# One piece of the probability split of the last batch on VectorE instead of GpSimd, in a cross-attention kernel

## The reference

```python
q, k, v = heads(layernorm(x) @ w_q), heads(ctx @ w_k), heads(ctx @ w_v)
scores = where(mask, -inf, q @ k.T / 8)
x = x + merge(softmax(scores) @ v) @ w_o
x = x + layernorm(x) @ quantized(kernel) + bias + (layernorm(x) @ a) @ b
```

## Time and profile before

| what | value |
|---|---|
| median of 3 runs | 502.15 us (498.56 to 502.39) |
| span of the profiled execution | 499.3 us |
| busy share of PE, DVE, ACT, POOL | 90%, 81%, 66%, 80% |
| granted TensorE clock, mean | 0.979 of full speed |

### The profile page before, as it was taken

How to read it: one execution, slowest core, us unless ns; L and a number is a source line. 1 busy time by engine, 2 the same in 40 slices (tenths; PEclk the granted TensorE clock), 3 DMA queues, 4 the chain that set the end, 5 groups by cost and what they waited for, 6 DMA issues and landing times.

```text
span 499.3 us, 15466 instructions
## 1 busy us (share of the span) xinstructions
PE 451.8 (90%) x5855; PEld 328.7 (66%) x5855; DVE 406.2 (81%) x1110; ACT 327.6 (66%) x845; POOL 398.7 (80%) x659
## 2 busy tenths in 40 slices
PE   3968989999999999999999999999999999888874
PEld 1434756777766866777766866687667867576662
DVE  4986779987988989788988989898988888778662
ACT  5967566875677766776677766776667666656530
POOL 5687478999788977788788978798797977889931
PEclk9999799999999999999999999999999999899897
DMA  8602685798957996689857985798677877669950
GB/s 284 213 23 43 125 178 113 137 182 169 168 115 144 196 144 118 123 185 161 145 116 141 195 158 119 144 182 160 129 141 128 158 143 142 126 126 177 155 127 27
DMA packets 218817, 71.91 MB, mean 144 GB/s; under 512 B 202785, under 2 KB 216882, under 8 KB 218738
## 3 DMA queue, kind: packets, MB, share of 16 engines
q1 hardware_dynamic: 217680, 69.25, 71.4%
q0 software_dynamic: 480, 1.31, 0.9%
q10 hardware_dynamic: 578, 0.30, 0.2%
HBM read 14.71 MB, written 4.19 MB: 38 GB/s over the span
## 4 chain that ended last, share of the span: by engine, by line
PE 43%; DVE 27%; ACT 16%; POOL 8%; issue 4%; DMA 2%; SPq 0%; DVEq 0%; POOLq 0%; ACTq 0%
PE ps_b L915 32%; ACT arena L673 8%; DVE ps_a L803 7%; PE ps_a L983 6%; DVE arena L796 4%; DVE arena L785 2%; ACT arena L652 2%; DVE arena L871 2%; DMA arena<-in_L_xattn_w_q_dram 2%; POOL arena L580 2%; PE ps_b L1035 2%; POOL arena L584 2%; PE ps_b L1004 2%; ACT arena L664 1%; DVE arena L807 1%
## 5 line engine op out<-in xcount | busy, mean ns | idle before, releaser
L915 PE MATMUL ps_b<-arena 128*128 128x65 f16 (+3 forms) x3348 | 323.6, 249 | 6.1 <-DVE arena L871 3.4
L915 PEld LDWEIGHTS ps_b<-arena 128*128 128x128 f16 x3348 | 224.5, 99 | 81.8 <-issue 6.1
L673 ACT ACTIVATE arena<-ps_a,arena 128x160 f32<-128x160 f32 x512 | 160.0, 396 | 92.6 <-DVE arena L807 84.0
L584 POOL TENSOR_TENSOR arena<-arena 128x512 f16<-128x512 f32 x128 | 148.6, 1161 | 0.0
L580 POOL CAST arena<-arena 128x512 f16<-128x512 f32 x128 | 78.4, 613 | 54.4 <-ACT arena L673 53.1
L803 DVE TENSOR_REDUCE ps_a<-ps_a 128x4 f32<-128x640 f32 x128 | 105.3, 822 | 0.0
L983 PE MATMUL ps_a<-arena 64*128 64x160 f16 x1536 | 76.2, 232 | 13.2 <-ACT arena L673 13.2
L983 PEld LDWEIGHTS ps_a<-arena 64*128 64x128 f16 x1536 | 50.8, 95 | 38.2 <-issue 20.9
L1004 PE MATMUL ps_b<-arena 128*128 128x65 f16 x512 | 72.1, 194 | 0.0
L871 DVE TENSOR_TENSOR arena<-ps_b,arena 128x256 f32<-128x256 f32 x128 | 54.3, 424 | 4.4
L796 DVE TENSOR_TENSOR arena<-ps_b,arena 128x512 f16<-128x512 f32 x60 | 41.1, 686 | 19.1 <-ACT arena L664 17.8
(11 more groups left out here) (139 smaller groups left out, 424.3 us busy)
## 6 DMA issues: line engine op xcount, KB each, us to landing
arena<-in_x_dram SPq DMA_DIRECT2D x8, 512.0 KB, 5.5
mask_u<-in_x_dram SPq DMA_DIRECT2D x32, 128.0 KB, 3.0
out_dram<-mask_u SPq DMA_DIRECT2D x32, 128.0 KB, 2.6
arena<-arena SPq DMA_TRANSPOSE x128, 4.0
arena<-arena SPq DMA_DIRECT2D x24, 65.0 KB, 2.7
arena<-in_L_xattn_w_q_dram SPq DMA_DIRECT2D x1, 1024.0 KB, 8.7
arena<-in_L_xattn_w_k_dram SPq DMA_DIRECT2D x1, 1024.0 KB, 10.7
arena<-in_L_xattn_w_v_dram SPq DMA_DIRECT2D x1, 1024.0 KB, 12.2
```

The source lines that it names most:

```text
L584: nc.gpsimd.tensor_tensor(lo_main, main, hi_main, ALU.subtract)
L673: ins = nc.scalar.activation(probs[k % 2][:, h, :], p_scores[k % 2][:, h % 2, h // 2 * WINDOW:(h // 2 + 1) * WINDOW], ACT.Exp, bias=neg_ma ...
L915: mm = nc.tensor.matmul(dst, a, c, start=(first and at == 0), stop=(last and at == n - 1))
```

## The change

In slots 112 to 127 POOL leaves out the low half of rest. Its split ends with the low half of main, and `p_lo_made` is raised there. DVE makes the low half of rest at the end of its slot k, behind the late items of the slot before. It waits for both high halves of k (`p_hi_made`) and raises a new semaphore, `rest_lo_made`. In these slots SP waits for both semaphores before it turns k, and ACT waits for both of k-2 before it writes `probs`. All other slots are as before.

```diff
+        DVE_RESTS = LAST - NS
             def turn_probs(k):
                 sp.wait_ge(p_lo_made, k + 1)
+                rests_low_by_dve(sp, k)
...
+        def rests_low_by_dve(eng, k):
+            if k >= DVE_RESTS:
+                eng.wait_ge(rest_lo_made, k - DVE_RESTS + 1)
...
                 pool.wait_ge(p_hi_made, 2 * k + 1)
-                nc.gpsimd.tensor_tensor(lo_main, main, hi_main, ALU.subtract)
-                pool.wait_ge(p_hi_made, 2 * k + 2)
-                nc.gpsimd.tensor_tensor(rests[:, :, 2, :], rest, rests[:, :, 0, :], ALU.subtract).then_inc(p_lo_made, 1)
+                ins = nc.gpsimd.tensor_tensor(lo_main, main, hi_main, ALU.subtract)
+                if k < DVE_RESTS:
+                    pool.wait_ge(p_hi_made, 2 * k + 2)
+                    ins = nc.gpsimd.tensor_tensor(rests[:, :, 2, :], rest, rests[:, :, 0, :], ALU.subtract)
+                ins.then_inc(p_lo_made, 1)
...
                     act.wait_ge(p_lo_made, k - 1)
+                    rests_low_by_dve(act, k - 2)
...
+                if DVE_RESTS <= s.k < LAST:
+                    rests = rest_parts(s.k % HALF_BUFS)
+                    dve.wait_ge(p_hi_made, 2 * s.k + 2)
+                    nc.vector.tensor_tensor(rests[:, :, 2, :], probs[s.k % 2][:, :, P:WINDOW], rests[:, :, 0, :],
+                                            ALU.subtract).then_inc(rest_lo_made, 1)
```

More of the change, by code:

```diff
@@ L311, in xattn_ffn @@
         p_lo_made = sem("p_lo_made")
+        rest_lo_made = sem("rest_lo_made")
         turned = [sem(f"turned{i}") for i in range(TURN_BUFS)]
@@ L543, in fast_sp, with rest_parts @@
                 sp.wait_ge(out_stored[i], 16 * (NT // 2 + 1))
+        def rest_parts(i):
+            return p_half[i][:, 2].rearrange("p e (c k) -> p e c k", c=P // REST)
+        def rests_low_by_dve(eng, k):
+            if k >= DVE_RESTS:
+                eng.wait_ge(rest_lo_made, k - DVE_RESTS + 1)
         def gather(b):
@@ L565, in norm @@
                 nc.gpsimd.tensor_tensor(ln_shift, ln_minus, ln_rstd, ALU.mult).then_inc(ln_rstd_made, 1)
-            def rest_parts(i):
-                return p_half[i][:, 2].rearrange("p e (c k) -> p e c k", c=P // REST)
             def split_probs(k):
```

## The result

The changed kernel is slower: 506.77 us in the median of 4 runs (506.41 to 508.34) against 501.79 (498.56 to 502.39), a ratio of 1.0128 with a 95% interval of 1.0089 to 1.0167. I had forecast 505.3 on 502.15, a rise of 0.6%. By the two ratios the rise is twice that. The quotient of the two medians is lower, 1.0099, and lies within the interval; four runs of each kernel do not give it more closely.

A forecast was written before the change was run, and what follows sets the result against it. It took POOL as full in the last batch, then DVE's held chain as what POOL waits for: 2.8 us late at the exponentials of 125, plus 0.2 and 0.2, sum 3.2 on 502.15, 505.3 us; range 499.5 to 508.

The forecast's parts named there:

- the hold: Slots 119 and 123: DVE's new two-SBUF-input subtraction stands until POOL's L584 ends at 2.03 us after the split's start.
- the sum's second line: Slot 121: from the exponentials to `w` on DVE pass 5.14 us of PE work, as before the change.
- slots 112 to 114: The first new instructions meet POOL's gap ahead of 441.92 us and cost 0.1 us.
- two cycles, hold: POOL's splits 115 to 119 and 119 to 123: each cycle 11.95 instead of 11.07 us, 0.9 longer.
- two cycles, clock: Rival, chance 0.12: PE idles longer and loses 2.4 GHz in two `w`, adding 2 x 0.9 us, 507.1 us.
- exponentials of 125 after split 123: Slot 125: held DVE delays these exponentials behind POOL's split of 123 by 0.9 us; 2.8 us late in all.
- from there to the end: After the exponentials of 125: 0.2 us for slot 126's new instruction before a division, 0.2 for its later transpose.
- DVE's instruction: DVE's new 128-element subtraction in slots 112 to 127: 0.30 us alone, 0.21 us of DVE's queue per slot.
- the high of the two bounds: DVE's new instruction loses the whole of POOL's L584, up to T+2.03; the low bound was no loss.
- T+3.80: T is the start of POOL's split of 119; exponentials of 121 start 3.80 us after it, instead of 2.56.
- The place of the wait: Slot 119: DVE, done at T+0.73, waits for POOL's cast of the high half of rest, ending at T+0.96.
- The rival 'no hold': Chance 0.20: DVE's instruction runs unharmed beside L584, waiting only for the cast; 0.3 us gained, 501.8 us.

The follow-up runs named there:

- the repeat: The changed kernel, unaltered, measured a second time with more rounds against the kernel before: 507.91 us, ratio 1.0117 (1.0072 to 1.0162).
- The run with one SBUF input: Changed kernel with DVE's new subtraction replaced by an equally long bn_stats reading one SBUF input, low half not made: 498.71 us, 0.9961 of the kernel before.

## Why the prediction was wrong

The direction, the hold and its place were right. The size was off by a factor of two, and the step that failed is the sum's second line, which carried the 5.14 us from the exponentials to `w` on DVE over unchanged and so put the clock at nothing. In slot 121 of the changed kernel this stretch took 6.78 us (459.63 to 466.41):

```profile
459.63 1.25 ACT L684 ACTIVATE arena<-ps_a,arena 128x160 f32<-128x160 f32 x4 [1.32 <-DVE arena L818]
...
466.41 0.42 DVE L859 SCALAR_TENSOR_TENSOR arena<-ps_b,mask_u 128x256 f32<-128x256 f32 x1 [1.76 <-PE ps_b L931]
```

In the repeat, in slot 117, where `w` kept the 2.78, it took 5.14 (445.36 to 450.50), to the digit what I had. So the chain was right and its clock was not:

```profile
445.36 1.25 ACT L684 ACTIVATE arena<-ps_a,arena 128x160 f32<-128x160 f32 x4 [1.32 <-DVE arena L818]
...
450.50 0.42 DVE L859 SCALAR_TENSOR_TENSOR arena<-ps_b,mask_u 128x256 f32<-128x256 f32 x1
```

Point by point, on the profiled pair:

| term | predicted | measured |
|---|---|---|
| slots 112 to 114 | +0.1 | 0.0 (`w` of 113 slow in both) |
| two cycles, hold | +1.8 | +1.35 (2 x 0.68) |
| two cycles, clock | 0 (a rival, 0.12) | +3.2 |
| exponentials of 125 after split 123 | +0.9 | +0.9 (3.75 against 2.84) |
| from there to the end | +0.4 | +1.1 (33.47 against 32.38) |
| sum | 3.2 | 6.5 |

- **DVE's instruction.** 0.30 alone, 0.21 of the queue: measured 0.28 and 0.20.
- **The hold.** I took it from one row, L889, and chose the high of the two bounds. Right: the exponentials of 121 came at T+3.74, I had T+3.80. The Trainium skill's rule (SBUF — State Buffer, section "Who interferes with whom", and the table in "Summary: rules for kernel authors") says that a VectorE instruction with two SBUF inputs and a GpSimd one that reads SBUF block each other, the second to start until the first is finished. The runs agree with it: in the 40 ends behind POOL's, in the 0.93 that became 0.44 when the POOL instruction was halved, and in the 0.28 of an instruction with one SBUF input.
- **The place of the wait.** Here I was half right. I had DVE waiting at T+0.73 for the cast. Once POOL waits for `w`'s chain, DVE is always later, at T+1.30 (457.19), and meets L592 already running. No wait for the cast is left. It changes little, as the hold ends with L592 all the same. The cycle at full clock is 11.75 against my 11.95: 0.06 because the exponentials come at T+3.74, and 0.1 because POOL's root starts 0.08 us behind the statistics, where I had allowed 0.2.
- **The rival 'no hold'** was priced as if DVE's place at T+0.73 stayed. The run with one SBUF input shows 11.1 per cycle, no gain, where I had 10.78.
- **The clock.** I gave it 0.12 as a rival, with 2 x 0.9 on top, 507.1. The measured 506.77 lies next to that, partly by luck: in the profiled pair the clock took 3.2 and not 1.8, and the hold 1.35 and not 1.8. My argument against it was that the clock was 1.00 with PE busy 0.81. But other windows of the last batch had 0.83, 0.91 and 0.92, and the `w` of 113 and 125 were slow in the kernel before. It should have been in the sum with a share: 0.8 us more idle PE in each cycle did not bring the low clock every time, but in four of six cases. In 10 runs of the changed kernel the mean clock was 0.967, in the 85 later ones of the kernel before 0.977.
- **The tail.** 0.4 predicted, 1.1 found. Of that the `w` of slot 129 is 1.4 more and that of 125 0.8 less, both the clock, so about 0.5 is the change's own. The instruction of 126 was held too (0.71), and PE waited 1.6 us for its transpose. The forecast 0.4 for this part was right.

Profile and runs do not share out the cost alike. In the profiled pair the clock is 3.2 of the 6.5 us. By the mean clock of many runs it is some 3 of 7, and some 4 us remain, more than the 3.3 that the other rows of the table add up to. What the difference is stays open.

The time between span and launch is a point that I got wrong as well. I took the profiled execution's time as its span. The runs later showed about 3.0 us around the span in the kernel before and 1.8 in the changed one, so the change costs about 1.2 us more in spans than in medians. Why it differs was not tried and stays open.

## What to carry to other kernels

Moving a small elementwise piece from GpSimd to VectorE is not a matter of the two engines' loads alone. With both its inputs in SBUF it was held here to the end of the GpSimd subtraction or cast that was running, and everything behind it in VectorE's queue with it. Compare it with an instruction of the same length and one SBUF input, and look for recorded durations that differ between instances of one instruction.

When a change adds idle time of TensorE ahead of its longest run of matmuls, price that run at both clocks and put the low one into the sum with a share. Here the same 24 matmuls cost 2.78 or up to 4.89 us, behind waits that were nearly the same. In the profiled pair that was half of the cost.

## What the runs showed that I had not expected

- Ten to fourteen matmuls that nobody needs, ahead of each `w`, made the kernel before 0.4% faster, and 21 per cycle took about 4 us off the changed one.
- The scatter between runs of one kernel goes with the clock: of the 85 later runs of the kernel before, the 17 at a mean of 0.969 have spans of 499.9 to 500.8 us, the 25 at 0.982 or over 494.9 to 498.2.
- The time outside the span was the same to about 0.5 us within each kernel, but near 3.0 us in some kernels, 1.8 in others and 3.6 in one.
